# A decoder kernel's distance attention: key norms with two moving columns, and a unit's second half of scores issued in pairs

## The reference

```python
P = X @ W_in + b_in                       # b, t, 16 heads x (Q, K, V, G) x 64
q2 = jnp.sum(Q * Q, axis=-1)
k2 = jnp.sum(K * K, axis=-1)
qk = jnp.einsum('hbtd,hbsd->hbts', Q, K)
d2 = q2[..., :, None] + k2[..., None, :] - 2.0 * qk
W = jnp.power(1e-4 + jnp.sqrt(jnp.maximum(d2, 0.0)), -2)
W = W / (1e-4 + jnp.sum(W, axis=-1, keepdims=True))
A = jnp.einsum('hbts,hbse->hbte', W, V)
return (G * A) @ W_out + b_out            # heads side by side
```

## Time and profile before

| | us |
|---|---|
| runs before | 1263.98 median of 3 (1263.01 to 1266.08) |
| the profiled execution, its own time | 1266.25 |
| its span in the trace | 1264.4 |
| TensorE (PE) busy | 1128.7, 89% |
| VectorE (DVE) busy | 904.6, 72% |
| ScalarE (ACT) busy | 879.9, 70% |
| GpSimd (POOL) busy | 628.3, 50% |

### The profile page before, as it was taken

The page is one execution under the profiler, slowest core; times in us unless marked ns, Lnnn a source line. Parts: engine busy times, 40 slices in busy tenths (PEclk is TensorE's granted clock), DMA queues, the critical chain, the costliest instruction groups (busy, mean ns, idle before and its releaser), DMA issues.

```text
span 1264.4 us, 17047 instructions
## 1 busy us (share of the span) xinstructions
PE 1128.7 (89%) x6055; PEld 588.6 (47%) x6055; DVE 904.6 (72%) x1756; ACT 879.9 (70%) x1150; POOL 628.3 (50%) x463
## 2 busy tenths in 40 slices
PE   6999999999999999987888888799997999985765
PEld 3444444444444444432233332277775676653444
DVE  6776667766766677657888978546746786878885
ACT  2999999999989998992666767655564677733411
POOL 2877777777766777694454645014330300054232
PEclk9999999999999999996889989999998999997877
DMA  7200000000000000020000000000001000000000
GB/s 177 68 1 1 1 1 1 1 1 1 1 1 1 1 1 1 1 68 1 18 1 1 1 1 1 2 1 1 1 2 63 1 1 1 1 1 0 1 9 25
DMA packets 25695, 14.48 MB, mean 11 GB/s; under 512 B 14622, under 2 KB 24460, under 8 KB 25484
## 3 DMA queue, kind: packets, MB, share of 16 engines
q1 hardware_dynamic: 25612, 13.39, 3.8%
HBM read 12.34 MB, written 1.05 MB: 11 GB/s over the span
## 4 chain that ended last, share of the span: by engine, by line
PE 32%; POOL 31%; issue 20%; DVE 15%; ACT 1%; POOLq 0%; DMA 0%; ACTq 0%; DVEq 0%
DVE ARENA L1170 6%; POOL ARENA L2729 6%; POOL ARENA L2727 6%; POOL ARENA L2723 6%; PE PS L1041 5%; POOL WQ L2740 3%; POOL ARENA L2753 3%; PE PS L911 3%; PE PS L1425 2%; PE PS L1015 2%; PE PS L843 2%; PE PS L1449 2%; PE PS L1416 2%; PE PS L859 2%; POOL WQ L2742 2%
## 5 line engine op out<-in xcount | busy, mean ns | idle before, releaser
L2579 DVE TENSOR_SCALAR ARENA<-PS,ARENA 128x512 f32<-128x512 f32 x256 | 174.6, 745 | 55.8 <-PE PS L2216 55.2
L1170 DVE TENSOR_REDUCE ARENA<-PS 128x1 f32<-128x512 f32 x256 | 160.9, 684 | 28.1 <-PE PS L859 27.6
L1086 ACT ACTIVATE ARENA<-PS 128x1024 f32<-128x1024 f32 x128 | 128.9, 1026 | 61.8 <-PE PS L897 61.5
L2397 ACT ACTIVATE ARENA<-ARENA 128x2048 f32<-128x2048 f32 x64 | 122.2, 1912 | 59.1 <-DVE ARENA L2579 58.8
L2216 PE MATMUL PS<-ARENA 64*128 64x512 f32 x512 | 130.2, 628 | 0.0
L2404 ACT ACTIVATE ARENA<-ARENA,consts_sb 128x2048 f32<-128x2048 f32 x64 | 124.7, 1996 | 0.4
L2226 PE MATMUL PS<-ARENA 128*64 128x512 f32 x512 | 118.6, 605 | 1.3 <-issue 1.3
L2410 ACT ACTIVATE ARENA<-ARENA 128x2048 f32<-128x2048 f32 x64 | 118.5, 1900 | 0.0
L1351 POOL TENSOR_TENSOR ARENA<-ARENA 128x512 f32<-128x512 f32 x32 | 40.7, 1273 | 121.4 <-DVE ARENA L1309 120.9
L2736 POOL TENSOR_SCALAR WQ<-ARENA,consts_sb 128x512 bf16<-128x512 f32 x32 | 22.3, 696 | 153.2 <-DVE ARENA L2555 153.2
L859 PE MATMUL PS<-ARENA 32*128 32x512 bf16 x256 | 73.6, 412 | 25.2 <-DVE ARENA L1170 20.0
(11 more groups left out here) (301 smaller groups left out, 2631.7 us busy)
## 6 DMA issues: line engine op xcount, KB each, us to landing
ARENA<-in_window_bias_dram SPq DMA_DIRECT2D x1, 1536.0 KB, 6.3
WKVG<-in_L_attn_W_in_dram SPq DMA_DIRECT2D x3, 384.0 KB, 5.5
X<-in_x_dram SPq DMA_DIRECT2D x4, 256.0 KB, 3.8
W<-in_L_ffn_w_dram SPq DMA_DIRECT2D x1, 1024.0 KB
out_dram<-X SPq DMA_DIRECT2D x4, 256.0 KB, 2.3
BV<-in_L_attn_b_in_dram SPq DMA_DIRECT2D x1, 512.0 KB, 6.5
Wout<-in_L_attn_W_out_dram SPq DMA_DIRECT2D x1, 512.0 KB, 4.6
WQ<-in_L_attn_wq_dram SPq DMA_DIRECT2D x1, 512.0 KB, 3.4
```

The source lines that it names most:

```text
L1086: act.activation(PT[m % PT_SLOTS], bank(("cP", m)), ACT.Exp, scale=0.5).then_inc(sem("c_exp"), 1)
L1170: dve.tensor_reduce(NMX[:, w % 2, t, h:h + 1], bank(("cS", n, j)), AX.X, ALU.max, negate=True).then_inc(sem("c_max"), 1)
L2397: act.activation(chunk(u, half), chunk(u, half), ACT.Sqrt).then_inc(sem("rooted"), 1)
L2579: dve.tensor_scalar(D[:, u % 2, kt, hd, :], bank(("S", u, c)), K2[:, u % 2, kt, hd:hd + 1], 1e-30, ALU.add, ALU.max).then_inc(sem("guarded ...
```

## The change

There are three edits. In `key_norms` on TensorE the moving operand is columns 0 and 64 of `pairsum` instead of all 128, so each of the four matmuls writes two columns. VectorE's copy reads the eight columns that now stand side by side. In `scores`, the second half goes out as tiles 4 and 5 (two pieces, two products) and then tiles 6 and 7 (two pieces, two products). The first half, the bank order and all semaphores stay.

```diff
                 for kt in range(QT):
-                    mm = pe.matmul(o[:, kt * P:(kt + 1) * P], KSQ[:, kt * P:(kt + 1) * P], const("pairsum"),
+                    mm = pe.matmul(o[:, 2 * kt:2 * kt + 2], KSQ[:, kt * P:(kt + 1) * P], const("pairsum")[:, ::64],
                                    start=True, stop=True)
...
-                for c in range(4 * half, 4 * half + 4):
-                    g = slice(32 * (2 * (c % 2) + c // 2 % 2), 32 * (2 * (c % 2) + c // 2 % 2) + 32)
-                    banks[c] = begin(("S", u, c))
-                    pe.matmul(banks[c], PIECES[g, :], STKQ[g, u % 2, :], start=True, stop=False)
-                for c in range(4 * half, 4 * half + 4):
-                    kt, hd = divmod(c, 2)
-                    r = slice(64 * hd, 64 * hd + 64)
-                    done(pe.matmul(banks[c], SK[r, u % 2, kt * P:(kt + 1) * P], MQ[r, u % 2, :], start=False, stop=True),
-                         ("S", u, c))
+                for group in ((0, 1, 2, 3),) if half == 0 else ((4, 5), (6, 7)):
+                    for c in group:
+                        g = slice(32 * (2 * (c % 2) + c // 2 % 2), 32 * (2 * (c % 2) + c // 2 % 2) + 32)
+                        banks[c] = begin(("S", u, c))
+                        pe.matmul(banks[c], PIECES[g, :], STKQ[g, u % 2, :], start=True, stop=False)
+                    for c in group:
+                        kt, hd = divmod(c, 2)
+                        r = slice(64 * hd, 64 * hd + 64)
+                        done(pe.matmul(banks[c], SK[r, u % 2, kt * P:(kt + 1) * P], MQ[r, u % 2, :], start=False, stop=True),
+                             ("S", u, c))
...
-                dve.tensor_copy(K2[:, u % 2], bank(("k2", u)).rearrange("p (k h e) -> p k h e", k=QT, h=2)[:, :, :, 0]
+                dve.tensor_copy(K2[:, u % 2], bank(("k2", u))[:, 0:2 * QT].rearrange("p (k h) -> p k h", k=QT)
                                 ).then_inc(sem("k2_sb"), 1)
```

## The result

| | median of the runs, us | lowest to highest | ratio to before, 95% interval |
|---|---|---|---|
| before | 1264.68 (6 runs) | 1262.98 to 1266.29 | |
| changed kernel | 1254.95 (6 runs) | 1253.11 to 1257.88 | 0.9922 [0.9912, 0.9931] |

The change makes the kernel faster by 9.7 us; the interval of the ratio gives 8.7 to 11.1. The forecast was 8.2 us faster and 1255.8. The profiled execution took 1253.11, with a span of 1251.3.

A forecast was written before the change was run, and what follows sets the result against it. TensorE was taken to set the pace from unit 2 to 29. The terms 6.2 + 3.0 - 1.0, with 0 for the key norms, gave 8.2 us off the median of 1263.98, so 1255.8, range 1251 to 1261.

The forecast's parts named there:

- TensorE binds from unit 2 to 29: In units 2 to 29, whatever shortens TensorE's own stream shortens the unit equally, until another engine binds.
- Two groups cost 2.76, the net is 0.28: Second half of an ordinary unit's scores: 3.04 us becomes 2.76; a wait of 0.79 goes, a second round of 0.51 comes.
- 22 ordinary units: Units 2, 4 to 9, 11 to 17, 19, 21 to 25, 27, 29: each gains 0.28 us, together 6.2.
- 4 units with a late guard, 3.0 us: Units 3, 10, 18 and 26, where VectorE comes late to guard 0: 0.75 us gained each, together 3.0.
- Units 20 and 28, -1.0: VectorE later still, no wait in the second half: they pay the second round of 0.51 us, together -1.0.
- Key norms, 0: Key norm matmuls on TensorE: the weight load sets the pace, so fewer moving columns gain 0 us.
- the 1.05 that was to be seen: Sign in the profile after: the eight key norm records still last 1.05 us.
- The estimate by the Trainium skill's table of spacings: Key norm matmuls with fewer moving columns would be spaced closer: 0.25 us a unit and 7 us in all.
- The sum, 8.2: Whole kernel: 6.2 + 3.0 - 1.0 = 8.2 us faster, with key norms and units 0, 1, 30, 31 at nothing.
- The forecast had allowed 3 for it: Rival, later stages: their clock falls land elsewhere and give some gain back, within 3 us of the forecast; no chance given.

The follow-up runs named there:

- pairs in both halves: The changed kernel with the first half of the scores also in pairs (tiles 0 and 1, then 2 and 3): 1268.54 us, ratio 1.0027 to the kernel before.
- halves: The changed kernel with each key norm matmul split into two of 64 stationary columns, side by side in the array: 1251.93 us, ratio 0.9891 to the kernel before.
- pairs alone: The changed kernel with the two key norm edits taken back, so only the second half's pairs remain: 1253.25 us, ratio 0.9910 to the kernel before.
- key norms alone: The kernel before with only the two moving columns and the copy that goes with them, score tiles as before: 1265.62 us, ratio 1.0005.
- changed kernel again: The changed kernel measured once more, nothing altered: 1255.75 us, ratio 0.9920 to the kernel before.

## Why the prediction was right, point by point

- **TensorE binds from unit 2 to 29: right.** In ordinary units 0.51 added to TensorE's stream came out whole (pairs in both halves), and so did 0.13 taken away (halves).
- **Two groups cost 2.76, the net is 0.28: right.** Measured 2.76, and 0.29 from unit to unit. The rule of the Trainium skill (TensorEngine Tiling, Key Properties) that a change of tiling drains the engine fits the added 0.51, which pairs in both halves show by itself. The runs show the price of the round, not that a drain makes it.
- **22 ordinary units: 20 of them.** Unit 2 gained 0.12. Up to K it is 0.50 shorter, of which 0.22 lie in its first half, but its row sums, which now wait for GpSimd, start 0.33 later behind K. Unit 4 lost 0.19: before, ScalarE's copy of a transpose ended 0.08 before the first piece; now its fourth piece waits for that bank, and the pieces are 0.79 ahead of the products instead of 0.33. The forecast had checked the banks that the guards free, not this one.

```profile
84.29 0.86 PE L2213 MATMUL PS<-ARENA,PIECES 32*128 32x512 bf16 x4
85.08 1.99 PE L2217 MATMUL PS<-ARENA 64*128 64x512 f32 x8
```

- **4 units with a late guard, 3.0 us: right.** They gained 0.89, 0.77, 0.70 and 0.70, together 3.1. With the ordinary ones the 26 units without 20 and 28 came down from 436.8 to 428.1 us, 8.7 against the forecast's 9.2.
- **Units 20 and 28, -1.0: the reading behind it is wrong, and it isn't one number.** -2.5 in the first profile, +0.8 in the second and in that of the pairs alone. The forecast took the late guard for the reason why nothing is waited for in their second halves. In the rows of the kernel before, from which it made the term, the clock had fallen in both units (granted clock 0.57 and 0.53 over their first products). Where it stayed high, the wait of 0.27 was there, and pairs gained 0.28 as in an ordinary unit: 3.04 against 2.76 in unit 20. Unit 28, where the clock stayed high in the key norms alone (in fours) and in the changed kernel again (in pairs), is 19.55 and 19.26 long.
- **Key norms, 0: right**, though not with the 1.05 that was to be seen: the records last 0.95 and give 0.08 back behind them. The estimate by the Trainium skill's table of spacings (TensorE: Matmul & The Clock Gate, Back-to-back issue gap), 7 us, is not what the runs show: the key norms alone came out at a ratio of 1.0005. The same page of the Trainium skill (LDWEIGHTS) has the weight load go by its columns. With 128 columns the distance of 0.11 between records agrees, and half of the columns took less, 0.56 in place of 0.81.
- **The sum, 8.2 against 9.7: near, with luck in it.** Three kernels with this second half were 9.7, 9.4 (the change again) and 11.3 us faster (pairs alone) by their medians. What their profiled executions took less than the profiled one before lies in these places (minus is more time):

| us less than before | up to unit 2 | the 26 units | units 20 and 28 | from unit 30 on | whole span |
|---|---|---|---|---|---|
| changed kernel, first profile | 1.3 | 8.7 | -2.5 | 5.7 | 13.1 |
| changed kernel again | 0.9 | 6.0 | 0.8 | -0.4 | 7.3 |
| pairs alone | 0.3 | 8.8 | 0.8 | 5.5 | 15.4 |

The 8.7 and the 8.8 are what the forecast has a mechanism for. In the second row the clock fell in unit 2 too (granted clock 0.50 over its first half). The last stretch is untouched by the change, and yet from the end of the last row sums on it took 683.2, 689.6 and 683.2 us in these three, and 689.4 before: one kernel differs from itself by more than 6 us there. The forecast had allowed 3 for it. Whether all of the 1.5 between forecast and median is of that kind, the runs don't settle.

## What to carry to other kernels

When an engine waits for a buffer at the head of a group, splitting the group frees what stands behind the wait, and costs another round of set-up; here both were read from the group's own records before the edit was made, and the 2.76 came out to the hundredth. Then walk down every buffer of the group, not only those that the waits name today: a bank that is free 0.1 us early becomes the next wait when the stream gets shorter. When a price is read from a row, look at the clock of that row: a unit at the low clock hid the wait that the change removes. The short matmuls with a wide stationary operand were shortened here by their stationary side, not by their moving one.

## What was not expected of the hardware

- Eight float32 records with 128 stationary and two moving columns free the engine 0.08 us earlier than with 128 moving columns (0.81 against 0.89), and the first record with 128 moving columns behind them takes that much longer (0.19 against 0.11).
- Sixteen records with 64 stationary columns on two halves of the array take 0.56 us, eight with 128 take 0.81.
- The width isn't all of it. The eight records of L825 also load 128 stationary columns, but from a single partition and for transposes, and they start 0.06 apart. No run here tells which of the two makes them shorter.
- A wait of 1.8 us of TensorE was followed by products at 1.2 GHz in one execution (3.41 us in unit 20 before) and at 2.4 GHz in another (1.99 us in unit 28 of the changed kernel run again).
